# Graph layer kernel on one core: the norm of x two chunks ahead, table stores on GpSimd, biases turned on TensorE, weights loaded behind the first edge lists

## What is computed

```python
agg = segment_sum(layernorm(x)[src], dst)             # 100000 edges + 6250 loops, N = 6250 nodes, 256 wide
h = relu(agg @ W_rel + b_rel + xn @ W_root)           # 512 wide
i, f, g, o = split(h @ W_ih.T + b_ih + b_hh)          # f is not used
c = sigmoid(i) * tanh(g)
x = x + (sigmoid(o) * tanh(c)) @ W_fc + b_fc
# second layer, on layernorm(x):
sw = softmax((xn @ W_x + b_x) @ W_slice + b_slice, over 64 slices, 8 heads, with a temperature)
tok = sums of (xn @ W_fx + b_fx) by sw ; attention of the 64 tokens of a head ; x = x + (back by sw) @ W_out + b_out
```

## Time and profile before

| | us |
|---|---|
| median of 3 runs (1571.45 to 1578.38) | 1572.49 |
| the profiled execution | 1571.3 |
| its span | 1567.9 |
| POOL: gathers L545, busy | 894.2 |
| PE busy | 1247.5 |
| first gather begins | 87.18 |
| last gather begins | 1369.44 |

### The profile page before, as it was taken

The page is one execution under the profiler, slowest core; times in us unless marked ns, Lnnn a source line. Parts: engine busy times, 40 slices in busy tenths (PEclk is TensorE's granted clock), DMA queues, the critical chain, the costliest instruction groups (busy, mean ns, idle before and its releaser), DMA issues.

```text
span 1567.9 us, 24946 instructions
## 1 busy us (share of the span) xinstructions
PE 1247.5 (80%) x8343; PEld 1076.1 (69%) x8343; DVE 823.2 (53%) x2125; ACT 583.1 (37%) x1120; POOL 941.0 (60%) x975
## 2 busy tenths in 40 slices
PE   0236788789888898889888988898889988895696
PEld 0224677678777787668776877687777777784596
DVE  3752264456455655555555545664556455544364
ACT  3621243434342444244423443343434342443132
POOL 1256677677677666767766666676767666600043
PEclk9998899999999999999999999999999999996599
DMA  5754334334434343434343434344343434302396
GB/s 157 237 174 117 108 108 120 116 116 114 128 111 126 104 127 110 121 107 124 113 124 104 128 115 122 105 127 121 117 118 113 129 112 125 108 27 63 101 347 208
DMA packets 109101, 198.02 MB, mean 126 GB/s; under 512 B 39587, under 2 KB 66079, under 8 KB 109052
## 3 DMA queue, kind: packets, MB, share of 16 engines
q0 software_dynamic: 46160, 124.60, 27.4%
q1 hardware_dynamic: 59312, 60.26, 13.3%
q10 hardware_dynamic: 3600, 12.80, 2.2%
HBM read 165.56 MB, written 32.87 MB: 127 GB/s over the span
## 4 chain that ended last, share of the span: by engine, by line
POOL 45%; DMA 20%; issue 20%; PE 9%; DVE 3%; SPq 1%; ACT 1%; POOLq 1%; DVEq 0%; ACTq 0%
POOL ring L545 45%; DMA ring<-table,sidx 17%; PE ps L296 2%; PE ps L298 2%; PE ps L297 2%; DMA table<-ring 1%; DMA ring<-dstp 0%; SPq L337 0%; PE ps L929 0%; ACT ring L609 0%; DVE stats L1070 0%; DMA ring<-in_x 0%; DMA ring<-in_b_fx 0%; PE ps L917 0%; POOLq L565 0%
## 5 line engine op out<-in xcount | busy, mean ns | idle before, releaser
L545 POOL DMA_INDIRECT ring<-table,sidx x900 | 894.2, 994 | 404.4 <-issue 299.3
L845 PE MATMUL ps<-ring,oneh 128*125 128x512 f16 x900 | 263.3, 429 | 164.4 <-DMA ring<-table,sidx 163.2
L296 PE MATMUL ps<-h_h,wih_h 128*128 128x256 f32 x1200 | 346.8, 289 | 0.5 <-DVE h_l L1261 0.5
L297 PE MATMUL ps<-h_l,wih_h 128*128 128x256 f32 x1200 | 339.7, 283 | 0.0
L298 PE MATMUL ps<-h_h,wih_l 128*128 128x256 f32 x1200 | 339.6, 283 | 0.0
L845 PEld LDWEIGHTS ps<-ring,oneh 128*125 128x125 f16 x900 | 123.4, 150 | 261.8 <-DMA ring<-table,sidx 215.8
L296 PEld LDWEIGHTS ps<-h_h,wih_h 128*128 128x128 f32 x1200 | 230.3, 192 | 4.2 <-issue 1.1
L297 PEld LDWEIGHTS ps<-h_l,wih_h 128*128 128x128 f32 x1200 | 230.4, 192 | 1.8
L298 PEld LDWEIGHTS ps<-h_h,wih_l 128*128 128x128 f32 x1200 | 230.2, 192 | 0.0
L675 ACT ACTIVATE gate<-ps,bgate 128x256 f32<-128x256 f32 x300 | 125.4, 469 | 220.4 <-PE ps L298 220.2
L1178 DVE TENSOR_SCALAR oneh<-iota,rel 128x125 f16<-128x125 f16 x900 | 157.8, 285 | 5.1 <-issue 3.4
(11 more groups left out here) (208 smaller groups left out, 2618.5 us busy)
## 6 DMA issues: line engine op xcount, KB each, us to landing
ring<-table,sidx POOLq DMA_INDIRECT x900, 2.8
swt_d<-swt ACTq DMA_DIRECT2D x25, 500.0 KB
gate<-swt_d SPq DMA_DIRECT2D x19, 500.0 KB, 5.8
ring<-in_x SPq DMA_DIRECT2D x12, 512.0 KB, 5.4
table<-ring SPq DMA_DIRECT2D x12, 512.0 KB, 5.4
xn<-table SPq DMA_DIRECT2D x25, 224.0 KB
xin<-in_x SPq DMA_DIRECT2D x25, 224.0 KB
res<-xin SPq DMA_DIRECT2D x25, 224.0 KB
```

What stands on the lines that cost most here:

```text
L296: eng.matmul(dst, wh, xh, start=first, stop=False)
L297: eng.matmul(dst, wh, xl, start=False, stop=False)
L545: pool.indirect_dma_start(ring[:, e, j, :], None, table, bass.IndirectOffsetOnAxis(ap=sidx[:, e, j:j + 1], axis=0)).then_inc(done, 16)
L845: last = pe.matmul(ps[0:WN, SUM_A + e, :], oneh[:, e, j, 0:WN], ring[:, e, j, :], start=(j == 0), stop=(j == CH - 1))
```

## The change

- On ACT the root of chunk k + 2 is taken behind the scaling of chunk k, and DVE takes the statistics of chunk k + 2 behind the scales of chunk k. `lx` keeps three buffers, `ln` two; `lt` gets a third, in `raw`.
- SP loads x only, the first chunk ahead of the copies of `dst` and `src`. POOL takes the low part of chunks 0 to 10 and stores each; it also issues the pads and the loads of the list as rows. SP stores chunk 11 and the rest, whose low parts DVE takes.
- `plan_a` to `plan_d` stand behind chunks 4, 6, 9 and 11 on DVE (before 1, 3, 8 and 10).
- `W_rel`, `W_root`, all biases, `W_slice` and `W_x` are loaded behind `edges(0, 0)` and `edges(0, 1)`. The 32 bias rows are loaded as rows (`brows`), turned by one TensorE transpose and copied to `bcols`.
- On DVE the split of `W_rel` and `W_root`, `bias_rows` and `slice_weights` stand behind the first one-hots; on PE the fold of `W_x` stands behind the plan and the flag's branch.

```diff
+        lt.append(raw[:, 4 * HID:4 * HID + words].bitcast(F16)...)
+        def lt_of(k):
+            return lt[k % 3] if k < NCH else rest16
@@ SP
-            (the copies of src and dst, ahead of load_chunk(0))
             load_chunk(0)
+            sp.dma_start(dstp[0:E]..., a["dst"]...).then_inc(ld_edges, 16)
             load_chunk(1)
             load_chunk(2)
-            (14 loads: b_rel, b_ih, b_hh, b_x, b_fc, b_out, b_slice, temperature, W_slice; W_x; pads; list rows)
+            sp.dma_start(srcp[0:E]..., a["src"]...).then_inc(ld_edges, 16)
             for k in range(NCH + 1):
                 if k + 3 <= NCH:
                     load_chunk(k + 3)
-                if k >= 1:
-                    store_chunk(k - 1)
...
+            for k in (NCH - 1, NCH):
+                store_chunk(sp, k)
...
             edges(0, 0)
             edges(0, 1)
+            sp.dma_start(r4[:, 0:CT, :], a["W_rel"]...).then_inc(ld_w1, 16)
+            sp.dma_start(r4[:, CT:2 * CT, :], a["W_root"]...).then_inc(ld_w1, 16)
+            for n, v in enumerate([a[b][g * HID:(g + 1) * HID] for b in ("b_ih", "b_hh") for g in GATES]
+                                  + [a["b_rel"], a["b_x"]]):
+                sp.dma_start(brows[KT * n:KT * n + KT, :], v.rearrange("(k p) -> k p", p=P)).then_inc(ld_small, 16)
...
+            sp.dma_start(wx_raw, a["W_x"].rearrange("(k p) n -> p k n", p=P)).then_inc(ld_wx, 16)
             sp.wait_ge(w1_free, 2)
+            for q in range(3):
+                sp.wait_ge(ln_out[q], 16 * len(range(q, NCH - 1, 3)))
+            sp.wait_ge(ln_last, 32)
@@ POOL
+            def low_chunk(k):
+                ln_low(pool, k)
+                store_chunk(pool, k)
+            low_chunk(0)
+            low_chunk(1)
+            (waits for ld_edges and ld_pads, loads of the list as rows)
+            for k in range(2, 6):
+                low_chunk(k)
             pool.wait_ge(plan_v, 3)
             pool.indirect_dma_start(edge_i[0:NW + 1, 0:ER], ...)
+            for k in range(6, NCH - 1):
+                low_chunk(k)
@@ ACT
             ln_dev(0)
+            ln_dev(1)
             for k in range(NCH + 1):
...
-                if k < NCH:
-                    ln_dev(k + 1)
+                if k + 2 <= NCH:
+                    ln_dev(k + 2)
-                if 2 <= k < NCH:
-                    act.wait_ge(ln_out[q], 16 * (k // 2))
+                if 3 <= k < NCH:
+                    act.wait_ge(ln_out[k % 3], 16 * (k // 3))
@@ PE
+            pe.wait_ge(ld_small, 16 * NSMALL)
+            pe.transpose(ps[:, 0, 64:64 + 8 * KT], brows, ident[0:8 * KT, 0:8 * KT])
@@ DVE
             def bias_rows():
+                dve.wait_ge(wxt_t, 1)
+                link(dve.tensor_copy(bcols[:, :], ps[:, 0, 64:64 + 8 * KT]))
...
             hots(0, 0)
+            (split of W_rel and W_root)
+            bias_rows()
+            slice_weights()
             for n in range(MT):
```

More of the change, by code:

```diff
@@ L217, in build_program @@
         ln_in = [sem(f"ln_in{k}") for k in range(3)]
-        ln_out = [sem(f"ln_out{k}") for k in range(2)]
+        ln_last = sem("ln_last")
+        ln_out = [sem(f"ln_out{k}") for k in range(3)]
         consts, dve_step, pe_step, pool_step = (
@@ L328, in _ @@
             load_chunk(0)
+            sp.dma_start(dstp[0:E].rearrange("(a b) -> a b", b=ER), a["dst"].rearrange("(a b) -> a b", b=ER)).then_inc(ld_edges, 16)
             load_chunk(1)
             load_chunk(2)
[L332 to L337, removed]
-                sp.dma_start(bxc, a["b_x"].rearrange("(k p) -> p k", p=P)).then_inc(ld_small, 16)
@@ L339, in _ @@
-            sp.dma_start(bfc[:, :], a["b_fc"].partition_broadcast(P)).then_inc(ld_small, 16)
-            sp.dma_start(bout[:, :], a["b_out"].partition_broadcast(P)).then_inc(ld_small, 16)
-            sp.dma_start(bsl, a["b_slice"].partition_broadcast(P)).then_inc(ld_small, 16)
-            sp.dma_start(temp8[:, :], a["temperature"].rearrange("a h b c -> (a h b c)").partition_broadcast(P)).then_inc(ld_small, 16)
-            for k in range(2):
-                sp.dma_start(wsl[k * D:(k + 1) * D, :], a["W_slice"]).then_inc(ld_small, 16)
@@ L355, in _ @@
-            sp.dma_start(edge_i[0:WN, 0:ER], rows).then_inc(ld_tab, 16)
-            with nc.allow_non_contiguous_dma(reason="one element a row"):
-                sp.dma_start(edge_i[0:WN, ER:ER + 1], nxt[:, 0:1]).then_inc(ld_tab, 16)
-            r4 = raw[:, 0:4 * HID].rearrange("p (k n) -> p k n", n=HID)
+            sp.dma_start(srcp[0:E].rearrange("(a b) -> a b", b=ER), a["src"].rearrange("(a b) -> a b", b=ER)).then_inc(ld_edges, 16)
             for k in range(NCH + 1):
@@ L494, in build_program @@
         NCONST = 8
+        NSMALL = 8 + 3 + 1 + 2
         def ln_low(eng, k):
@@ L529, in _ @@
             pool.memset(pick[:, :], 0.0).then_inc(consts, 1)
-            ln_low(pool, 1)
-            ln_low(pool, 3)
+            pool.wait_ge(pads_set, 2)
+            for idx, t in ((sidx, srcp), (didx, dstp)):
+                pool.dma_start(t[E:EP].rearrange("(p b) -> p b", p=P), idx[:, 0, :]).then_inc(ld_pads, 16)
+            def low_chunk(k):
[3 more added lines that the diff above has]
+            low_chunk(1)
+            pool.wait_ge(ld_edges, 32)
+            pool.wait_ge(ld_pads, 32)
+            rows = dstp[0:E].rearrange("(p b) -> p b", b=ER)
+            nxt = dstp[ER:E + ER].rearrange("(p b) -> p b", b=ER)
+            pool.dma_start(edge_i[0:WN, 0:ER], rows).then_inc(ld_tab, 16)
+            with nc.allow_non_contiguous_dma(reason="one element a row"):
+                pool.dma_start(edge_i[0:WN, ER:ER + 1], nxt[:, 0:1]).then_inc(ld_tab, 16)
+            for k in range(2, 6):
+                low_chunk(k)
             pool.wait_ge(plan_v, 3)
```

136 lines of the change are left out of this document (64 added, 72 removed).

## The result

The changed kernel takes 1597.54 us (median of 4 runs, 1594.16 to 1604.54) against 1575.43 of the kernel before in the same session (4 runs, 1571.45 to 1581.74): a ratio of 1.0142 (95% interval 1.009 to 1.0194), some 22 us slower. The forecast was 1573.0 with a range of 1564 to 1582, "no change": it is wrong, and the result is outside the range. The profiled execution took 1596.32, its span is 1594.6.

The account below looks back on a forecast made before the run. The prediction took POOL's gathers, running at their own pace, to bound the kernel. 1571.3 - 8.0 (earlier first gather) + 9.4 (POOL's stand ahead of gather 37) = 1572.7, given as 1573.0 us, range 1564 to 1582.

Parts of the forecast that it names:

- The first gather: End of the norm: POOL's first gather starts 8.0 us earlier, at 79.2 instead of 87.18.
- the rounds of two chunks: Norm on ACT: 10.1 us from the end of scaling k to that of k + 2, 5.05 a chunk, set by loads.
- the waits behind the plan: Norm, chunk 11: `plan_c` and `plan_d` on DVE delay its scaling by 1.7 us, between nothing and 3.5.
- Stores on POOL: Norm on POOL: subtraction of 2.12 us and a store's issue, 2.8 to 3.5 a chunk, hidden by the wait for loads.
- The rival of slow stores: Norm on POOL: a store takes 3.1 us, a chunk 5.2, adding about 3.5 to the norm: 1576; chance 0.06.
- The chain of the weights: From the first list to pair 1's lists, 61.1 us of serial steps; POOL stands 9.4 us ahead of gather 37.
- The cover: First 36 gathers: POOL has its own 51.7 us of work between the first gather and gather 37.
- What is behind gather 37 stays as it is: Gather loop from gather 37, the first of pair 1, to the last: no change in time from the edit.
- fixed stretch: Gathers on POOL: they run at their own pace, so the time is the first gather's start (87.18 us) plus a constant.
- A rule against the change: POOL's stores beside DVE's 2-port modes might take 3.1 us; loop waits of 1.7 and 1.9 us at most spoke against starving.
- the four rivals: Quick loads 1568.5 us (chance 0.15), hidden weights 1563.3 (0.12), slow small loads on SP 1581 (0.17), slow POOL stores 1576 (0.06).
- The landing of 3.2 us: Loads of x in the norm: the skill's 2.0 us plus bytes over 436 GB/s; first gather then about 13 us earlier.

Follow-up runs that it names:

- e4: The changed kernel with ACT's root and DVE's statistics one chunk ahead instead of two: 1583.79 us, ratio 1.0106 to the kernel before.
- e1: The kernel before with 40 empty semaphore increments at the start of POOL's program, gather loop at instruction 157: 1591.66 us, ratio 1.0166 to the kernel before.
- e2: The changed kernel with 88 empty semaphore increments at the start of POOL's program, gather loop at instruction 245: 1576.06 us, ratio 1.0042 to the kernel before.
- e7: The changed kernel with three semaphore increments on DVE in each turn, ahead of the two `hl_l`: 1593.57 us, ratio 1.0097 to the kernel before.
- e8: The changed kernel with norm one ahead, small loads and weights' work ahead of the flag, 88 empty increments on POOL: 1571.84 us, ratio 0.9964 to the kernel before.

## Why the prediction was wrong

- **The first gather: right, with some luck.** 79.2 was said, 77.69 measured. The pairs came as described, if less evenly (chunks 5 and 6 are scaled 3.1 apart at 37.00 and 40.11, chunk 7 5.8 later), and chunk 11 was scaled at 65.23 (66.9 said), with ACT's root waiting for DVE, and DVE for the load. Two terms were off and cancelled in part: the rounds of two chunks up to the end of chunk 8 took 10.0, 9.6 and 9.1 where 10.1 was said, and the waits behind the plan took 2.32 and 2.79 where 1.7 in all was said. That two ahead costs time is confirmed by e4: 11.7 us as against one.
- **Stores on POOL: right.** A chunk is 2.12 for the subtraction, 0.57 of idle time and 0.57 for the issue, 3.3 in the forecast's 2.8 to 3.5, hidden by the loads. The rival of slow stores didn't come: no store took over 0.6 us.
- **The chain of the weights: right.** `W_x` was issued 9.75 behind the first list (10.4 said) and landed at 90.63, 6.9 later (6.0), the fold took 10.8 (10.8), the lists of pair 1 went out 61.0 behind the first (61.1). POOL stood for 7.37; gather 37 is 60.3 behind the first, 8.6 more than before (9.4 said). The cover was not as it was taken: POOL stood 4.70 for its own gathers after the first nine.
- **The sum up to gather 37: right to 2.3 us**: -0.9 where +1.4 was said.
- **"What is behind gather 37 stays as it is": wrong**, and with it the "fixed stretch" of the first paragraph. This is the step that failed: a term of +26.6 us that the sum had at nothing. The earlier trace rows shows only what POOL waits for between instructions, and by them the stretch is indeed fixed. What lies inside an instruction does not show in the waits: the mean of 994 ns beside 0.95 us of most gathers held 41.6 us already in the kernel before. I took the gather's duration for its own. The same reading of waits stands in "A rule against the change", where waits of 1.7 and 1.9 us were to show that nothing held the descriptors in the loop. None of the four rivals had this; the two that forecast more time rested on SP's and POOL's issues and would not have led there.
- **The cause** is shown in part. That the place of POOL's loop sets the phase, and the phase the held gathers, is shown by e1 and e2, from both sides: +1.66% with the change's place in the old kernel, and a ratio of 1.0042 in place of 1.0142 with another place in the new one. That DVE's two-operand instructions hold the gathers is shown by e7 and by the count over both profiles. In the profiled executions e2 takes back 20.1 of the 26.6 us, e1 brings 16.6. Why the jump back takes 0.13 us more at 157 is not known. The rest, 6.5 us in e2, is 3.0 in held gathers (44.6 us against 41.6), and the clean pitch is the likely other part (4.5 ns by some 740 clean gathers is 3.3 us), its cause open. Without both the forecast of no change would have held nearly: in e2's profiled execution the last gather starts 6.1 us behind that of before.
- **The rule weighed.** The rows show that a store's issue on POOL took 0.57 and that indirect gathers were held by 0.2 to 1.0 us beside DVE's products of two SBUF operands, and not beside one-hots with one. The Trainium skill (SBUF — State Buffer, "Who interferes with whom") says that such a DVE instruction contends with what GpSimd reads in SBUF, and that a DVE instruction with one input, outside the 2-port modes, does not; there the trace agrees: none of 79 gathers beside one with an operand in PSUM was held. It infers besides that `tensor_tensor` does not stall a DMA of GpSimd, as descriptors need the write side. The gathers here, whose indices lie in SBUF, differ from that: 1.44 to 1.97 us against 0.95. I weighed the rule on the eleven stores, where it cost nothing, and not on the 900 gathers. The landing of 3.2 us that the prediction weighed beside it and set aside did not come: the loads of x landed in 4.9 us in the median, where 4.8 was kept.

## What to carry to other kernels

Where one engine issues hundreds of like instructions on the path, compare their mean with the shortest of them: the difference is time that no list of waits shows, and what runs on the neighbour engine at the start of the long ones names the cause. A loop whose turns lock two engines together can gain or lose a per cent by a shift of 0.1 us, and the shift can come from code that runs once, far ahead of it; so before a change of a prologue is judged by the total time, look whether its own stretch did what it should, and shift the loop by empty instructions to see what is the edit and what the phase. And an earlier start is not an earlier end: e8 was 9.9 us ahead at gather 37 and level at the last.

## What the runs showed of the hardware

- The issue of an indirect transfer by GpSimd, 0.95 us, is longer (1.97 in the longest row shown) when it starts while VectorE works on two fp32 operands in SBUF, and then ends 0.81 to 0.84 us after that has ended (185 cases in two profiles). A gather that starts up to 0.04 us behind VectorE's start, or ahead of it, is not held; in e7 the VectorE instruction was 0.05 longer then. With one operand in SBUF (one-hots, a reduction, a sum whose other operand is in PSUM) it stays at 0.94 to 0.95.
- The idle time of GpSimd's sequencer at the jump back of a loop depended on where the loop stood in its program: 1.66 us with the loop at instruction 117, 1.76, 1.79 and 1.85 at 157, with the same code in it.
- Chips differ in what they grant TensorE: 0.924 and 0.88 to 0.90 for this work, with 1569 to 1580 us for the kernel before on some and 1722 to 1784 on others. At the lower one the kernel has another bound, PE with 42 to 53% of the chain in place of 9%.
